# Channel attention's logits, exponential and scaling one slot earlier, in the slots of a fused two-layer attention kernel

## What is computed

```
# layer 0, channel attention, 8 heads of 24 channels, N = 1024 pixels
qkv = w_qkv @ xf + b_qkv                      # xf: (B, 192, N)
q = q / |q| ; k = k / |k|                     # norms over the N pixels
attn = softmax((q @ k.T) * temperature)       # per head, 24 x 24
x = x + (w_proj @ (attn @ v) + b_proj)
# layer 1, on tokens t = x as (B, 1024, 192)
t = t + causal_attention(layernorm(t))        # 6 heads of 32
t = t + ffn(layernorm(t))                     # 192 -> 768 -> 192, sign weights, quantised in groups of 6 images
```

## Time and profile before

| what | value |
|---|---|
| median of 3 runs | 4539.35 us |
| lowest and highest | 4538.74 and 4539.68 us |
| profiled execution, its time | 4540.19 us |
| profiled execution, its span | 4538.4 us |
| mean granted TensorE clock | 0.977 of full speed |

### The profile page before, as it was taken

How to read it: one execution, slowest core, us unless ns; L and a number is a source line. 1 busy time by engine, 2 the same in 40 slices (tenths; PEclk the granted TensorE clock), 3 DMA queues, 4 the chain that set the end, 5 groups by cost and what they waited for, 6 DMA issues and landing times.

```text
span 4538.4 us, 114718 instructions
## 1 busy us (share of the span) xinstructions
PE 4010.0 (88%) x39240; PEld 2939.7 (65%) x39240; DVE 3043.9 (67%) x5559; ACT 2975.3 (66%) x6669; POOL 363.7 (8%) x374
## 2 busy tenths in 40 slices
PE   6999988879999888999998879999888999898887
PEld 4767665667777646777665667777646777665665
DVE  5666666766666667666766766666666666766765
ACT  3666666657776655666676667776655676676666
POOL 1000002000000110000002000000110000002000
PEclk7999999999999999999999999999999999999999
DMA  2111111011221101111111011211101111111011
GB/s 72 37 37 36 43 36 29 1 50 36 54 47 36 36 0 43 36 37 36 43 36 29 1 50 38 57 42 36 36 0 43 37 36 41 39 36 29 1 43 43
DMA packets 48640, 161.00 MB, mean 35 GB/s; under 512 B 12420, under 2 KB 12934, under 8 KB 48006
## 3 DMA queue, kind: packets, MB, share of 16 engines
q1 hardware_dynamic: 48134, 154.39, 14.2%
HBM read 28.52 MB, written 25.17 MB: 12 GB/s over the span
## 4 chain that ended last, share of the span: by engine, by line
PE 63%; DVE 14%; issue 13%; ACT 6%; POOL 2%; DVEq 1%; DMA 1%; ACTq 1%; SPq 0%; POOLq 0%
PE PT L690 10%; PE OUT L710 10%; PE S L676 6%; DVE nmax L1213 5%; PE PT L808 5%; PE S L735 5%; PE S L634 3%; PE FR L634 3%; PE FR L578 2%; PE S L779 2%; ACT work L936 2%; DVE work L382 2%; DVE XT L1084 2%; PE FR L641 1%; PE S L641 1%
## 5 line engine op out<-in xcount | busy, mean ns | idle before, releaser
L1213 DVE TENSOR_REDUCE nmax<-S 128x1 f32<-128x256 f32 (+7 forms) x1536 | 1146.1, 753 | 937.0 <-PE S L678 927.0
L936 ACT ACTIVATE work<-S,nmax 128x256 f32<-128x256 f32 (+7 forms) x1536 | 1137.7, 742 | 613.9 <-DVE nmax L1213 594.8
L690 PE MATMUL PT<-ident,work 128*128 128x128 f32 x6912 | 1076.7, 280 | 93.2 <-DVE work L382 54.5
L690 PEld LDWEIGHTS PT<-ident,work 128*128 128x128 f32 x6912 | 748.2, 142 | 260.0 <-ACT work L928 54.3
L382 DVE COPY work<-PT 128x512 f32<-128x512 f32 x768 | 524.1, 682 | 45.0 <-PE PT L690 37.8
L928 ACT ACTIVATE work<-PT 128x256 f32<-128x256 f32 (+3 forms) x768 | 338.1, 440 | 153.6 <-PE PT L690 146.4
L676 PE MATMUL S<-KS,QS 128*128 128x512 f16 (+3 forms) x1152 | 323.5, 335 | 111.4 <-ACT work L936 76.9
L676 PE MATMUL S<-odd 128*128 128x512 f16 (+3 forms) x1152 | 315.5, 328 | 71.7 <-ACT work L936 68.0
L678 PE MATMUL S<-causal,identb 128*128 128x128 bf16 x1536 | 339.2, 221 | 0.0
L940 ACT ACTIVATE work<-PT 128x512 f32<-128x512 f32 (+3 forms) x768 | 332.4, 433 | 1.4 <-PE PT L690 1.4
L936 ACT ACTIVATION_READ_ACCUMULATOR work<-S,nmax 128x1 f32 x1536 | 304.6, 198 | 0.0
(11 more groups left out here) (208 smaller groups left out, 6113.6 us busy)
## 6 DMA issues: line engine op xcount, KB each, us to landing
X<-in_x SPq DMA_DIRECT2D x32, 768.0 KB, 5.3
odd<-hi_z SPq DMA_DIRECT2D x128, 192.0 KB, 4.2
odd<-odd SPq DMA_DIRECT2D x128, 192.0 KB, 4.3
out_y<-work SPq DMA_DIRECT2D x64, 384.0 KB, 4.0
QS<-hi_z SPq DMA_DIRECT2D x64, 192.0 KB, 3.9
QS<-odd SPq DMA_DIRECT2D x64, 192.0 KB, 4.1
KS<-hi_z SPq DMA_DIRECT2D x64, 192.0 KB, 4.6
KS<-odd SPq DMA_DIRECT2D x64, 192.0 KB, 4.7
```

The source lines that it names most:

```text
L690: last = tr(bank[:, P * (j - c0):P * (j - c0) + P], PS[m % 2][:, m // 2 % 2, P * j:P * j + P], ident[:, :])
L936: A(PS[n % 2][:, n // 2 % 2, 0:w], S[:, n % 2, 0:w], ACT.Exp, bias=nmax[:, n % MAXES:n % MAXES + 1], accum_out=rowsum[:, sum_col(n):sum_co ...
L1213: v.tensor_reduce(nmax[:, n % MAXES:n % MAXES + 1], S[:, n % 2, 0:P * (qtile(n) + 1)], AX.X, ALU.max, negate=True).then_inc(max_made, 1)
```

## The change

Two tables change. Four steps of the front are placed one slot earlier: rb on PE, logits on DVE, xexp on ACT and attn on DVE. The steps ahead of them (norms, rdiag) and behind them (u, mt) stay.

```diff
 SLOTS = {"xt0": 0, "xt1": 1, "xt2": 2, "xt3": 4, "g0a": 5, "g0": 6, "g1a": 7, "g1": 8, "wg0": 9, "wg1": 10,
-         "na": 11, "rb": 15, "u": 18, "mt": 19, "t0": 20, "t1": 21, "t2": 22, "t3": 23, "z0": 31, "z1": 32,
+         "na": 11, "rb": 14, "u": 18, "mt": 19, "t0": 20, "t1": 21, "t2": 22, "t3": 23, "z0": 31, "z1": 32,
...
-SMALL_SLOTS = {"norms": 12, "rdiag": 13, "logits": 16, "xexp": 17, "attn": 17.5, "ln_stats0": 22, "ln_stats1": 25,
+SMALL_SLOTS = {"norms": 12, "rdiag": 13, "logits": 15, "xexp": 16, "attn": 16.5, "ln_stats0": 22, "ln_stats1": 25,
```

## The result

The changed kernel takes 4556.1 us (4555.02 to 4558.22 in 6 runs) against 4539.05 us before (4538.1 to 4540.03 in 6 runs). The ratio is 1.0038, with a 95% interval of 1.0025 to 1.0051: it is slower by 17.0 us. The forecast was 4552.7.

What follows compares the result with a forecast made beforehand. A chain of hand-overs between PE, DVE and ACT in slots 14 to 19 bounds the stretch. Thirteen terms sum to 8.85 us against 8.42; 0.43 us over 31 fronts gives 13.3 us and 4552.7 us, range 4541 to 4566.

Steps and rivals of the forecast that it cites:

- rb: On PE, now ahead of the scores of unit 15: that unit's maximum starts 0.33 us later, bounds nothing and 0.49.
- the queue behind the scaling: On DVE, unit 17's maximum now stands behind the waiting scaling, at 1081.29 instead of 1079.34, with its exponential in turn.
- The other twelve terms: From unit 15's maximum to L719, the hand-overs on DVE and ACT that with rb's 0.33 sum to 8.85 us.
- The logits' 1.35: On DVE, the four logits instructions now run ahead of unit 16's maximum and take 1.35 us on the path.
- the exponential's 0.84: On ACT, channel attention's exponential until the scaling starts on DVE: 0.84 us.
- the scaling's 0.56: On DVE, from the scaling's start to the next maximum, now unit 17's: 0.56 us.
- the output copy's 0.46: On ACT, the copy of the attention output (L925) now stands on the path: 0.46 us, upper bound 0.57.
- The two waits: DVE's wait for the exponential at L1126 shrinks from 1.88 to 1.06 us; PE's 1.26 us at L610 goes.
- The delay is kept: At L719 on PE: the 0.43 us passes on through 13.00 us of unbroken PE work; nothing gives it back.
- Rival (B): No change that can be told: hidden slack absorbs the delay or rb slips into an issue gap, 4539.4 to 4542.5; chance 0.15.
- Rival (A): Faster: the gap at the scaling closes and nothing replaces it, 0.63 us shorter per front, 4519.9 us; chance 0.12.
- The rule of the DRAIN section: On DVE at L1123: a semaphore after each copy costs nothing extra, so the 0.16 us wait vanishes; estimate 4547.7 us.

## Why the prediction was right

The sign, the size and the steps held. Forecast +0.43 us for each front and 4552.7 us; measured +0.53 and 4556.1.

- **rb** was the term most under its value: 0.33 forecast, 0.39 measured (2.04 - 1.65), and 0.40 by rb alone and by the pairs of runs with and without it. The 0.33 was read in rb's old place; in the new one it takes 0.41 to the next start. It carried most of the loss: 0.40 of the 0.53 us. The rest costs 0.13 us by the chain (0.10 forecast), too little to tell in the time of its own run. The sum had already said so (0.33 of its 0.43), though its text put the weight on the queue behind the scaling. That queue is what ate the gain; rb is most of what the change costs beyond it.
- **The other twelve terms** summed to 8.52 us, and the changed trace gives 1087.57 - 1079.01 = 8.56. The logits' 1.35 came out at 1.34, the exponential's 0.84 at 0.85, the scaling's 0.56 at 0.56, the output copy's 0.46 at 0.48.
- **The two waits** behaved as said: 1.06 us forecast at L1126 and 1.01 measured, and the wait at L610 gone. Unit 17's maximum was forecast 1.95 us later and came 2.04 later.
- **The delay is kept**: 0.53 us at L719 and 0.53 in the period. Rival (B) falls with that.
- **Rival (A)**, the gain with nothing in its place, needed the exponential ready when VectorE comes for it. In this order it is not. It is where the scaling stays behind unit 17's maximum, and then the gain is there: 1.24 us by the scaling's place alone, and 1.51 us against the kernel before when rb and the logits stay too.
- **The rule of the DRAIN section** would have taken 0.16 us from the logits. The row of L1123 in the changed trace has the 0.16 us of wait again, and the estimate by the rule, 4547.7, lies 8 us below the result. The prediction stretched the rule: what the Trainium skill, page "VectorE: DVE Perf Modes", section "The DRAIN you can't avoid", gives there was measured on eight copies, and L1123 is a maximum that waits for the addition ahead of it (L1120).
- **What the prediction lacked** is the clock. It took every image to be like the one it read, while 8 of 25 periods before were about 1.0 or 1.65 us longer. In this change that came to little: 17.0 us measured against 16.4 by the chain. Nothing in the prediction said that it would; in other orders of the same steps it reached 16 us. So that the time came out this near to the chain's is partly luck. Had the clock taken 16 us here too, the time would have been near 4539 + 16 + 16 = 4571 us, outside the range given.

## What to carry to other kernels

In a program where each engine works in order, a shorter wait can be worth nothing if the waiting instruction moves ahead of others that were ready: put the producer earlier and leave the consumer behind the work that needs no wait. Here the producer (the exponential) alone gave 43 us. Producer and consumer (the scaling) together gave nothing by the chain, and cost 16 us with the falls of the clock. Before a short product is moved, look at who waits on the other side of its new place. Here its whole length went to that engine: 0.40 us for each front.

## What the runs showed of the hardware

TensorE's granted clock fell from 2.4 to 1.2 GHz for short parts of some images and not of others with the same instructions. The falls lie behind stretches in which the engine stood idle for about a microsecond at a time (1.26 us ahead of L610 in the kernel before), and in the long images at two places: behind slots 17 to 19 and behind slots 25 to 29. Such idle time does not always bring one: in the image of the earlier trace rows, where TensorE was idle for 2.48 of 9.00 us, none followed (clock 1.00 from 1085 to 1098 us), while the image at 540 us of the same trace has one at the same place. An image with both falls took 105.48 us against 102.81, 2.7 us more. Matmuls without any use took 20 us off one kernel, put into the idle time of slot 18, and 12 us off another, put into slots 25 to 29. The Trainium skill, page "TensorE: Matmul & The Clock Gate", section "A second HAM failure mode: psum-queue depth-cycling", tells of a kernel whose frequent short idles between groups of matmuls let the clock swing between its two levels. The traces agree in that: the mean clock of ten microseconds is 0.83 behind such idles in one image and 1.00 in another. Why one image falls and its neighbour doesn't is left open.
